# Cross-attention and MoE feed-forward: the q and k parts go into the score stacks straight from SBUF instead of through DRAM

## The chip, the cores and the metric

One core of a Trainium2 chip runs the whole kernel. The metric is device time in microseconds (us) for one execution, as the median of several runs. Engines are called TensorE (PE in the profile, with PEld for its weight loads), VectorE (DVE), ScalarE (ACT), GpSimd (POOL) and SyncE (SP). SyncE does no arithmetic: it issues the DMA transfers, one after the other, and a wait in its stream holds everything behind it.

## The reference

x and ctx have 16 batches of 128 rows of 256. The first layer is attention with 16 query heads of 16 and one shared key/value head:

```
x  = layernorm(x)
qh = (x @ w_q)  -> 16 heads of 16;   k, v = ctx @ w_kv   (16 each)
x  = x + concat_heads(softmax(qh k^T / 4) v) @ w_concat
```

The second is a top-1 mixture of 8 experts (256 -> 1024 -> 256, gelu, 256 rows of capacity each) beside a residual MLP of the same shape. The two outputs are mixed by a softmax of two learned coefficients and added to the residual. Everything is in f32, and the score product must keep nearly f32 accuracy.

## The kernel before

**Tiles.** The 16 batches make U = 8 tiles ("u") of T = 2 batches ("t"), 256 rows. A tile passes through layer norm, transposes, the k/v and q products, the scores, the softmax, PV, the projection, the gate, a scatter of its rows to the experts' slots in DRAM, and the residual MLP. After the last tile the 8 experts run.

**Stacks.** q and k are each split into three bf16 parts (high, middle, low), made in SBUF as `qpart` (128 partitions: 16 dimensions d times 8 head pairs h) and `kpart` (16 partitions). The six products of parts that matter are put side by side along the contraction: `qstack` and `kstack` have 96 = 6 x 16 rows of parts, row 16a + d holding dimension d of copy a, plus two rows for the running maximum. The high q part fills copies 0 to 2, the middle 3 and 4, the low 5; the k copies are 0, 1, 2, then 0, 1, then 0. One matmul over 96 rows then gives a score. The fold of 128 partitions (d, h) into 16 rows of 8 heads needs DMA.

**How the stacks are filled before.** `k_spill(u)` (L434) writes kpart to DRAM in three transfers. `q_spill(u, i)` (L445) waits for part i (q_hi, q_mid, q_parts) and writes it to DRAM, three, two and one times over, by one transfer each. `gather(u, i)` (L455) waits until those have landed (and, from tile 2 on, until the second scores of tile u - 2 no longer need the buffer), and reads all 96 rows of kstack by one transfer and of qstack by one for each of the two batches. All stacks and parts are double-buffered by u % 2.

**Who uses them.** `score_max` on TensorE (step "A", L696) multiplies groups g = 0 to 7 (four heads each, the first four groups for batch 0) and VectorE takes the maxima of each (L1064). The maxima are transposed (step "M", L708), negated and split in two, and `maxima` on SyncE (L467) puts them into the last two rows of qstack. Then `scores_T` (step "B", L718) computes the transposed scores, 98 rows deep, and ScalarE takes the exponential (L904). Tile 0 does its maxima in two halves, the others in one. `k_parts` on GpSimd (L548) and `q_first` on ScalarE (L882) overwrite kpart and qpart of the tile before last.

**Order.** There is no scheduler at run time. Every engine runs one fixed stream. The order of each stream is worked out when the kernel is built: each step has a planned time (tables AT0, AT1, AT for tiles 0, 1 and the rest, relative to the tile's own time OWN[u]) and each engine adds a lag per kind (LAG_SP for SyncE and so on); sorting gives the stream. On SyncE the resulting order around the first tiles is: loads, q_spill 0 of tile 0, k_spill of tile 0, q_spill 1 and 2, load of tile 3, gather 0 of tile 0, q_spill 0 and k_spill and q_spill 1 and 2 of tile 1, gather 1 of tile 0, gather 0 of tile 1, maxima of tile 0 (first half), gather 1 of tile 1, maxima of tile 0 (second half), load of tile 4, the zeroing of the experts' slots. From tile 4 on it is: maxima of tile u - 1, q_spills 0 to 2 of tile u, k_spill, the two gathers, then output rows, weights and a load.

On TensorE the order of tile 1's first scores is: second half of tile 0's A, M of tile 0, A 0 and 1 of tile 1, context transposes of tile 2, A 2 of tile 1, B 0 of tile 0, k/v product of tile 2, and on in this manner.

Of the kernel before, what the change touches and what calls it, by code (L numbers as in the profile page):

```python
# [5 lines left out]
def xattn_moe_ffn_kernel(nc, x, ctx, w_q, w_kv, w_c, nw, nb, wg, inter_w, inter_b, output_w, output_b,  # L6
# [4 lines left out]
    bf16 = mybir.dt.bfloat16  # L11
# [14 lines left out]
    T = 2  # L26
# [23 lines left out]
    out_v = out.rearrange("(b p) d -> b p d", p=P)  # L50


    dram_q = nc.dram_tensor("dram_q", [2, REP, P, KC * UT], bf16).ap()
    dram_k = nc.dram_tensor("dram_k", [2, REP, DH, UT], bf16).ap()
    disp = nc.dram_tensor("dispatched", [E * CAP + S, ROW], f32).ap()


# [3 lines left out]
    while len(OWN) < U + 3:  # L61
# [9 lines left out]
        "down": [0.08, 0.92, 1.12, 2.02, 7.51, 10.4, 27.63, 33.31], "kspill": [-40.85],  # L71
        "qspill": [-47.2, -43.78, -37.85], "gather": [-34.62, -27.72],
    }
    AT1 = {
        "load": [-99.9], "ln1": [-77.08], "xn": [-50.43], "ctxT": [-48.78], "xT": [-41.65], "kv": [-46.17],
# [5 lines left out]
        "down": [-2.72, -1.63, 2.04, 2.67, 8.58, 11.01, 13.67, 16.13], "kspill": [-26.77],  # L81
        "qspill": [-33.14, -29.81, -29.17], "gather": [-40.06, -39.06],
    }
    AT = {
        "load": [-98.82], "ln1": [-69.02], "xn": [-48.54], "ctxT": [-48.69], "xT": [-41.01], "kv": [-46.16],
# [5 lines left out]
        "down": [-3.91, -1.52, 1.85, 2.78, 6.17, 12.14, 13.12, 15.62], "kspill": [-25.95],  # L91
        "qspill": [-34.54, -33.37, -31.71], "gather": [-39.81, -38.61],
    }
    EARLY = 0.01
    LAG_PE = {
# [16 lines left out]
        "bias": [-5.5], "down": [0.38], "qlast": [-0.2], "end": [-0.84], "small": [-0.06], "ws1": [1.57],  # L112
    }
    LAG_SP = {
        "load": [-4.81], "kspill": [-5.64], "qspill": [-0.35], "gather": [13.54], "M": [3.71], "wload": [0.2],
        "ein": [1.22], "down": [7.99], "zero": [3.09], "late": [0.29], "w1load": [-0.02], "end": [-0.43],
        "small": [0.55], "w2load": [0.66],
    }
# [19 lines left out]
    for u in range(U):  # L138
        at = (AT0, AT1, AT)[min(u, 2)]
        for kind in ("load", "ln1", "xn", "ctxT", "xT", "kv", "q", "qrest", "qmid", "qlast", "vt", "oT", "proj", "ln2",  # L140
                     "core", "gate", "loc"):
            if kind != "load" or u >= 2:
                add(OWN[u] + at[kind][0], kind, u)
        free = OWN[u - 2] + 14.6 if u >= 2 else -100
        add(max(OWN[u] + at["kspill"][0], free), "kspill", u)
        for i, phase in enumerate(at["qspill"]):
            add(max(OWN[u] + phase, free + 0.1 * (i + 1)), "qspill", u, i)
        for i in range(T):
            add(max(OWN[u] + at["gather"][i], free + 0.5 + 0.1 * i), "gather", u, i)
        for i in range(T - HALVES[u], T):  # L150
            add(OWN[u] + at["M"][i], "M", u, i + HALVES[u] - T)
        for kind in ("A", "B", "PV", "part", "o"):
            for i, phase in enumerate(at[kind]):
                add(OWN[u] + phase, kind, u, i)
        weighed = max(OWN[u + 1] + at["gw"][0] if u + 1 < U else 0, OWN[u] + at["loc"][0] + 0.1)
        add(weighed, "gw", u)
        add(max(OWN[u + 1] + at["bias"][0], weighed + 0.1), "bias", u)
        for c, phase in enumerate(at["up"]):
            add(OWN[u + 1] + phase, "up", u, c)
        for i, phase in enumerate(at["down"]):  # L160
            t, q = divmod(i, 4)
            add(OWN[u + 1] + PERIOD + (phase if u >= 2 else at["down"][4 * t] + EARLY * q), "down", u, t, q)
# [23 lines left out]
    with ExitStack() as ex:  # L186
# [187 lines left out]
        def _(sp):  # L374
# [56 lines left out]
                w1load(e)  # L431
                w2load(e)

            def k_spill(u):  # L434
                r = u % 2
                sp.wait_ge(sem("k_parts"), u + 1)
                if u >= 2:
                    sp.wait_ge(sem(f"stack_in{r}"), 16 * (u // 2))
                row = 0
                for parts in (3, 2, 1):  # L440
                    sp.dma_start(dram_k[r, row:row + parts].rearrange("a d t -> d a t"), kpart[:, r, 0:parts, :])\
                      .then_inc(sem(f"k_spill{r}"), 16)
                    row += parts

            def q_spill(u, i):  # L445
                r, (name, row, times) = u % 2, (("q_hi", 0, 3), ("q_mid", 3, 2), ("q_parts", 5, 1))[i]
                sp.wait_ge(sem(name), u + 1)
                if u >= 2:
                    for t in range(T):
                        sp.wait_ge(sem(f"q_in{r}{t}"), 16 * (u // 2))  # L450
                sp.dma_start(dram_q[r, row:row + times].rearrange("a p c -> p a c"),
                             qpart[:, r, i, :, :, :].rearrange("p t m x -> p (t m x)").unsqueeze(1)
                             .broadcast_to([P, times, T * KC * P])).then_inc(sem(f"q_spill{r}"), 16)

            def gather(u, i):  # L455
                r = u % 2
                if i == 0:
                    if u >= 2:
                        sp.wait_ge(sem("b_done"), G * (u - 1))
                    sp.wait_ge(sem(f"k_spill{r}"), 3 * 16 * (u // 2 + 1))  # L460
                    sp.dma_start(kstack[0:KS, r, :], dram_k[r].rearrange("a d t -> (a d) t")).then_inc(sem(f"stack_in{r}"), 16)
                    sp.wait_ge(sem(f"q_spill{r}"), 3 * 16 * (u // 2 + 1))
                sp.dma_start(qstack[0:KS, r, i, :, :].rearrange("r (h m) x -> r h (m x)", m=KC),
                             dram_q[r].rearrange("a (d h) (t c) -> t (a d) h c", d=DH, t=T)[i])\
                  .then_inc(sem(f"q_in{r}{i}"), 16)

            def maxima(u, i):  # L467
                sp.wait_ge(sem("m_split"), max_steps(u, i) + 1)
# [24 lines left out]
            def end():  # L493
                sp.wait_ge(sem("acc_out"), 16 * (NBATCH + 1))

            calls = {"small": small, "late": late, "zero": zero, "load": load, "wload": wload, "w1load": w1load, "w2load": w2load, "kspill": k_spill, "qspill": q_spill, "gather": gather, "M": maxima, "ein": expert_in,
                     "down": down, "end": end}
            for step in order(LAG_SP):
                if step[0] in calls:
# [3 lines left out]
        def _(pool):  # L503
# [44 lines left out]
            def k_parts(u):  # L548
                pool.wait_ge(sem("kv_copied"), u + 1)
                if u >= 2:  # L550
                    pool.wait_ge(sem(f"k_spill{u % 2}"), 3 * 16 * (u // 2))
                k = kpart[:, u % 2, :, :]
                own(pool.tensor_copy(k[:, 0, :], kv32[0:DH, :]))
                own(pool.tensor_tensor(kres[:, :], kv32[0:DH, :], k[:, 0, :], ALU.subtract))
                own(pool.tensor_copy(k[:, 1, :], kres[:, :]))
                pool.tensor_tensor(k[:, 2, :], kres[:, :], k[:, 1, :], ALU.subtract).then_inc(sem("k_parts"), 1)
# [77 lines left out]
        def _(pe):  # L634
# [61 lines left out]
            def score_max(u, g):  # L696
                r, t, bs = u % 2, g // HG, slice((g // HG) * P, (g // HG + 1) * P)
                if g == 0:
                    pe.wait_ge(sem(f"stack_in{r}"), 16 * (u // 2 + 1))
                if g % HG == 0:  # L700
                    pe.wait_ge(sem(f"q_in{r}{t}"), 16 * (u // 2 + 1))
                b = claim("A", u, g)
                for i in range(4):
                    last = nc.tensor.matmul(b[:, i * P:(i + 1) * P], qstack[0:KS, r, t, 4 * (g % HG) + i, :],  # L704
# [147 lines left out]
        def _(act):  # L852
# [29 lines left out]
            def q_first(u):  # L882
                act.wait_ge(sem("q_done"), u + 1)
                if u >= 2:
                    act.wait_ge(sem(f"q_spill{u % 2}"), 3 * 16 * (u // 2))
                copy(qpart[:, u % 2, 0, :, :, :], by_batch(place["q", u])).then_inc(sem("q_hi"), 1)

            def q_second(u):
# [359 lines left out]
```

## Time and profile before

| | |
|---|---|
| median of 3 runs | 373.2 us (372.02 to 373.33) |
| the profiled execution | 374.39 us, span of the core 372.7 us |
| TensorE busy | 340.6 us, 91% of the span |
| VectorE / ScalarE / GpSimd busy | 56% / 58% / 43% |
| DMA: moved, mean rate | 49.83 MB, 134 GB/s |
| SyncE transfers for the stacks, per tile | 3 k spills, 3 q spills, 1 k gather, 2 q gathers |

The span is the time from the first to the last instruction of the core in the profile; the time of the execution also holds what lies around it. A row of a timeline has a start (us), a duration (us), the engine, the line of the kernel, the operation, the tile written and the tiles read, a count where several are merged, and in brackets how long the engine stood idle before and what ended that. For SyncE (SPq) the duration is that of the issue alone; the data lands later.

### The profile page before, as it was taken

The numbers are of one execution on the slowest core, as the hardware profiler recorded it, in microseconds if no ns is written. First come the engines' busy times: TensorE is split into PE (matmuls) and PEld (weight loads), VectorE is DVE, ScalarE is ACT, GpSimd is POOL, SyncE is SP. The second block draws the span as 40 slices with busy tenths as digits, with TensorE's granted clock in tenths as the row PEclk, the third lists the DMA queues.
The fourth block names the chain that finished last, engine by engine and source line by source line (L and its number), as shares of the span: only waits on it lengthen the run. The fifth ranks groups of instructions, "written<-read, shape, count | busy, mean of one in ns | idle before, by whom it ended". The sixth has DMA issues, their size and how long they took to land.

```text
span 372.7 us, 6349 instructions
## 1 busy us (share of the span) xinstructions
PE 340.6 (91%) x2234; PEld 277.6 (74%) x2234; DVE 207.8 (56%) x533; ACT 217.9 (58%) x397; POOL 160.5 (43%) x219
## 2 busy tenths in 40 slices
PE   3748889999999999999999989989999999999990
PEld 2425545875885885886786776778899999999990
DVE  4255528843762673574475462422668977878550
ACT  3311376484474465456447346363799999999730
POOL 4430233369657446636735542446002443334232
PEclk9965599999999999999999999999999999999996
DMA  6665539381224306706804400102936987875122
GB/s 183 197 202 144 166 106 315 117 230 60 79 82 116 99 28 179 261 2 176 288 2 133 107 2 15 44 1 66 295 84 182 279 272 189 233 199 140 17 30 28
DMA packets 51336, 49.83 MB, mean 134 GB/s; under 512 B 4765, under 2 KB 48489, under 8 KB 51305
## 3 DMA queue, kind: packets, MB, share of 16 engines
q1 hardware_dynamic: 48232, 45.21, 40.4%
q0 software_dynamic: 3072, 4.21, 6.1%
q8 instruction: 18, 0.29, 0.3%
q14 instruction: 14, 0.11, 0.1%
HBM read 33.65 MB, written 15.63 MB: 132 GB/s over the span
## 4 chain that ended last, share of the span: by engine, by line
PE 83%; DVE 5%; ACT 4%; issue 2%; DMA 2%; SPq 1%; POOL 1%; POOLq 0%; DVEq 0%
PE ubank L651 25%; PE mbank L833 16%; PE mbank L651 12%; PE mbank L646 4%; PE mbank L839 4%; PE mbank L840 4%; PE mbank L838 4%; PE pbank L736 4%; PE sbank L704 4%; PE sbank L726 4%; DVE smax L1069 2%; PE pbank L745 2%; DMA qstack<-dram_q 1%; DMA wq_raw<-in_L_xattn_w_q 1%; ACT h L976 1%
## 5 line engine op out<-in xcount | busy, mean ns | idle before, releaser
L976 ACT ACTIVATE h<-ubank,vecT 128x256 f32<-128x256 f32 x128 | 53.1, 467 | 29.8 <-PE ubank L651 29.7
L619 POOL DMA_INDIRECT out_rows<-yrow,rowid x16 | 32.3, 2017 | 74.0 <-DVE yrow L1213 74.0
L833 PE MATMUL mbank<-w2r,h 128*128 128x256 f32 x256 | 61.6, 383 | 1.5 <-ACT h L976 0.7
L651 PE MATMUL ubank<-ao,w1r 128*128 128x256 f32 x256 | 60.4, 382 | 0.0
L1069 DVE TENSOR_REDUCE smax<-sbank 128x4 f32<-128x512 f32 x64 | 42.5, 686 | 21.1 <-PE sbank L704 20.7
L833 PEld LDWEIGHTS mbank<-w2r,h 128*128 128x128 f32 x256 | 47.1, 190 | 9.3 <-issue 1.6
L651 PEld LDWEIGHTS ubank<-ao,w1r 128*128 128x128 f32 x256 | 46.8, 190 | 5.8
L910 ACT ACTIVATE p<-sbank 128x512 f32<-128x512 f32 x64 | 35.7, 596 | 15.7 <-PE sbank L726 15.5
L838 PE MATMUL mbank<-w2h,hh 128*128 128x256 f32 x128 | 36.4, 285 | 0.0
L840 PE MATMUL mbank<-w2h,hl 128*128 128x256 f32 x128 | 36.0, 281 | 0.0
L839 PE MATMUL mbank<-w2l,hh 128*128 128x256 f32 x128 | 36.0, 281 | 0.0
L704 PE MATMUL sbank<-kstack,qstack 96*128 96x128 bf16 x256 | 26.1, 236 | 5.9 <-DVE smax L1069 2.8
L704 PEld LDWEIGHTS sbank<-kstack,qstack 96*128 96x128 bf16 x256 | 19.3, 105 | 16.2 <-issue 6.5
L651 PE MATMUL ubank<-aoh,w1h 128*128 128x256 f32 x128 | 26.3, 286 | 0.0
L651 PE MATMUL ubank<-aol,w1h 128*128 128x256 f32 x128 | 25.6, 281 | 0.0
L651 PE MATMUL ubank<-aoh,w1l 128*128 128x256 f32 x128 | 25.6, 281 | 0.0
L568 POOL TENSOR_TENSOR yy<-va,mhalf 128x4 f32<-128x4 f32 x8 | 8.3, 1043 | 38.5 <-DVE va L1106 38.5
L839 PEld LDWEIGHTS mbank<-w2l,hh 128*128 128x128 f32 x128 | 24.2, 189 | 0.0
L838 PEld LDWEIGHTS mbank<-w2h,hh 128*128 128x128 f32 x128 | 24.2, 189 | 0.0
L840 PEld LDWEIGHTS mbank<-w2h,hl 128*128 128x128 f32 x128 | 24.2, 189 | 0.0
L726 PE MATMUL sbank<-qstack,kstack 98*128 98x512 bf16 x64 | 22.5, 396 | 1.6 <-ACT p L910 1.4
L1191 DVE TENSOR_TENSOR hl<-h,hh 128x512 fp32r<-128x512 f32 x32 | 21.9, 687 | 1.8 <-ACT hh L854 1.8
(139 smaller groups left out, 668.4 us busy)
## 6 DMA issues: line engine op xcount, KB each, us to landing
w1e<-in_L_ffn_inter_w SPq DMA_DIRECT2D x8, 1024.0 KB, 6.6
w2e<-in_L_ffn_output_w SPq DMA_DIRECT2D x8, 1024.0 KB, 7.9
qstack<-dram_q SPq DMA_DIRECT2D x16, 384.0 KB, 4.7
dram_q<-qpart SPq DMA_DIRECT2D x8, 384.0 KB, 2.6
dispatched<-zrow SPq DMA_DIRECT2D x4, 516.0 KB, 6.1
drow<-dispatched SPq DMA_DIRECT2D x8, 258.0 KB, 7.6
xs<-in_x SPq DMA_DIRECT2D x8, 256.0 KB, 3.2
ctxs<-in_ctx SPq DMA_DIRECT2D x8, 256.0 KB, 3.4
```

The lines of the kernel that those rows point to most:

```text
L619: pool.indirect_dma_start(out=out[:, :], in_=yrow[:, e % 2, t, :], in_offset=None, compute_op=ALU.add, out_offset=bass.IndirectOffsetOnAxi ...
L651: last = nc.tensor.matmul(dst, w[kc], v[kc], start=(kc == 0), stop=(kc == len(w) - 1))
L704: last = nc.tensor.matmul(b[:, i * P:(i + 1) * P], qstack[0:KS, r, t, 4 * (g % HG) + i, :], kstack[0:KS, r, bs], start=True, stop=True)
L726: nc.tensor.matmul(b[:, :], kstack[:, r, bs], qstack[:, r, t, hs:hs + 4, :], start=True, stop=True)\
L833: last = nc.tensor.matmul(b[:, 0:D], h[:, n % 2, f, t * P:(t + 1) * P], w2[:, f, :], start=(f == 0), stop=(f == FC - 1))
L838: nc.tensor.matmul(b[:, 0:D], hi, wh, start=(f == 0), stop=False)
L839: nc.tensor.matmul(b[:, 0:D], hi, wl, start=False, stop=False)
L840: last = nc.tensor.matmul(b[:, 0:D], lo, wh, start=False, stop=(f == FC - 1))
L910: nc.scalar.activation(p32[:, (k // HB) % 2, g % HB, :, :], scores, ACT.Exp, scale=SCALE)\
L976: nc.scalar.activation(h[:, n % 2, f, :], place["up", n, c][:, j, :], ACT.Gelu_apprx_tanh, bias=vecT[:, col:col + 1]).then_inc(sem("gelu_d ...
L1069: V.reduce_max(smax[:, g // HG, hs:hs + 4], place["A", u, g][:, :].rearrange("p (h t) -> p h t", h=4), AX)\
L1191: V.tensor_tensor(hl[:, n % 2, 2 * c:2 * c + 2, :], a, hh[:, n % 2, 2 * c:2 * c + 2, :].bitcast(f32), ALU.subtract)\
```

## The change

The two DRAM tensors go, and so does the step "gather". In the places of k_spill and q_spill in every order stand `k_stack` and `q_stack`, which write the stacks directly: 6 transfers of 8 KB for k and 6 + 4 + 2 transfers of 64 KB for q in each tile. The wait for the second scores of tile u - 2, which stood ahead of the gather, now stands ahead of these. The semaphores that TensorE waits for count six transfers, and k_parts and q_first wait for the stack transfers of tile u - 2 in place of the spills.

```diff
-    dram_q = nc.dram_tensor("dram_q", [2, REP, P, KC * UT], bf16).ap()
-    dram_k = nc.dram_tensor("dram_k", [2, REP, DH, UT], bf16).ap()
...
-        for i in range(T):
-            add(max(OWN[u] + at["gather"][i], free + 0.5 + 0.1 * i), "gather", u, i)
...
-            def k_spill(u):
-                r = u % 2
+            def k_stack(u):
+                r, row = u % 2, 0
                 sp.wait_ge(sem("k_parts"), u + 1)
                 if u >= 2:
-                    sp.wait_ge(sem(f"stack_in{r}"), 16 * (u // 2))
-                row = 0
+                    sp.wait_ge(sem("b_done"), G * (u - 1))
                 for parts in (3, 2, 1):
-                    sp.dma_start(dram_k[r, row:row + parts].rearrange("a d t -> d a t"), kpart[:, r, 0:parts, :])\
-                      .then_inc(sem(f"k_spill{r}"), 16)
-                    row += parts
-
-            def q_spill(u, i):
+                    for i in range(parts):
+                        sp.dma_start(kstack[row:row + DH, r, :], kpart[:, r, i, :]).then_inc(sem(f"stack_in{r}"), 16)
+                        row += DH
+
+            def q_stack(u, i):
                 r, (name, row, times) = u % 2, (("q_hi", 0, 3), ("q_mid", 3, 2), ("q_parts", 5, 1))[i]
                 sp.wait_ge(sem(name), u + 1)
                 if u >= 2:
+                    sp.wait_ge(sem("b_done"), G * (u - 1))
+                for a in range(row, row + times):
                     for t in range(T):
-                        sp.wait_ge(sem(f"q_in{r}{t}"), 16 * (u // 2))
...
+                        sp.dma_start(qstack[a * DH:(a + 1) * DH, r, t, :, :].rearrange("d (h m) x -> d h (m x)", m=KC),
+                                     qpart[:, r, i, t, :, :].rearrange("p m x -> p (m x)"))\
+                          .then_inc(sem(f"q_in{r}{t}"), 16)
...
-                    pool.wait_ge(sem(f"k_spill{u % 2}"), 3 * 16 * (u // 2))
+                    pool.wait_ge(sem(f"stack_in{u % 2}"), REP * 16 * (u // 2))
...
-                    pe.wait_ge(sem(f"stack_in{r}"), 16 * (u // 2 + 1))
+                    pe.wait_ge(sem(f"stack_in{r}"), REP * 16 * (u // 2 + 1))
                 if g % HG == 0:
-                    pe.wait_ge(sem(f"q_in{r}{t}"), 16 * (u // 2 + 1))
+                    pe.wait_ge(sem(f"q_in{r}{t}"), REP * 16 * (u // 2 + 1))
...
-                    act.wait_ge(sem(f"q_spill{u % 2}"), 3 * 16 * (u // 2))
+                    for t in range(T):
+                        act.wait_ge(sem(f"q_in{u % 2}{t}"), REP * 16 * (u // 2))
```

## Rows read from the trace of the kernel before

**Rows 1.** Page, 40 slices of the span: TensorE busy in tenths, and its granted clock.
```profile
PE   3748889999999999999999989989999999999990
PEclk9965599999999999999999999999999999999996
```

**Rows 2.** Chain that ended last, 0 to 70 us: start us, length us, what.
```profile
20.75 0.61 ACT qpart L854
...
24.37 3.99 DMA qstack<-dram_q
...
29.05 0.70 DVE smax L1069
```

**Rows 3.** Timeline of SyncE, tile 0: start us, issue us, line, operation.
```profile
13.03 0.37 SPq L451 DMA_DIRECT2D dram_q<-qpart  x1
...
14.57 0.42 SPq L441 DMA_DIRECT2D dram_k<-kpart  x1
...
16.02 0.45 SPq L410 DMA_DIRECT2D xs<-in_x  x1
...
17.66 0.66 SPq L463 DMA_DIRECT2D qstack<-dram_q  x1
```

**Rows 4.** By source line: issue ns min/median/max, and for two lines issue to landing.
```profile
L463 SPq DMA_DIRECT2D qstack<-dram_q x16: 547/616/1192, 17.7 to 202.9; - x16
...
DMA to landing us min/median/max: 4.0/4.7/6.3
...
L472 SPq DMA_DIRECT2D qstack<-nmax x14: 514/562/894, 47.3 to 221.6; - x14
...
DMA to landing us min/median/max: 1.8/1.9/2.2
...
L441 SPq DMA_DIRECT2D dram_k<-kpart x24: 312/420/1425, 13.4 to 200.4; - x24
```

**Rows 5.** Timeline of TensorE, tiles 0 and 1.
```profile
17.42 3.29 PE L651 MATMUL mbank<-xT,wq 128*128 128x256 f32 x8 [0.78 <-ACT xT L854]
22.03 0.61 PE L704 MATMUL sbank<-kstack,qstack 96*128 96x128 bf16 x8 [1.32 <-DMA qstack<-dram_q]
...
28.41 1.03 PE L704 MATMUL sbank<-kstack,qstack 96*128 96x128 bf16 x8 [1.50 <-DMA qstack<-dram_q]
...
32.05 1.06 PE L704 MATMUL sbank<-kstack,qstack 96*128 96x128 bf16 x8
...
34.23 0.59 PE L726 MATMUL sbank<-qstack,kstack 98*128 98x512 bf16 x1
```

**Rows 6.** Timeline: a q product at each clock; one window (clock, DMA share, GB/s last).
```profile
41.61 3.73 PE L651 MATMUL mbank<-xT,wq 128*128 128x256 f32 x8
...
64.84 1.95 PE L651 MATMUL mbank<-xT,wq 128*128 128x256 f32 x8
...
45.00:46.00 1.00, 0.78 (x6) 0.31 (x4) 0.41 (x1) 0.63 (x2) 0.00 (x0) 0.90 0.00 0
```

**Rows 7.** Timelines around tile 2's stack: second scores of tile 0, SyncE, first scores.
```profile
47.61 0.39 PE L726 MATMUL sbank<-qstack,kstack 98*128 98x512 bf16 x1 [0.47 <-ACT p L910]
...
48.61 1.44 SPq L441 DMA_DIRECT2D dram_k<-kpart  x3
...
59.77 0.40 PE L704 MATMUL sbank<-kstack,qstack 96*128 96x128 bf16 x4
```

**Rows 8.** Timelines of tiles 5 and 6: first q transfer on SyncE, first scores on TensorE.
```profile
138.01 0.52 SPq L451 DMA_DIRECT2D dram_q<-qpart  x1
...
150.92 0.39 PE L704 MATMUL sbank<-kstack,qstack 96*128 96x128 bf16 x4
...
166.65 2.79 SPq L451 DMA_DIRECT2D dram_q<-qpart  x3
...
179.85 0.39 PE L704 MATMUL sbank<-kstack,qstack 96*128 96x128 bf16 x4
```

More of the change, by code:

```diff
@@ L71, in xattn_moe_ffn_kernel @@
         "down": [0.08, 0.92, 1.12, 2.02, 7.51, 10.4, 27.63, 33.31], "kspill": [-40.85],
-        "qspill": [-47.2, -43.78, -37.85], "gather": [-34.62, -27.72],
+        "qspill": [-47.2, -43.78, -37.85],
     }
@@ L81, in xattn_moe_ffn_kernel @@
         "down": [-2.72, -1.63, 2.04, 2.67, 8.58, 11.01, 13.67, 16.13], "kspill": [-26.77],
-        "qspill": [-33.14, -29.81, -29.17], "gather": [-40.06, -39.06],
+        "qspill": [-33.14, -29.81, -29.17],
     }
@@ L91, in xattn_moe_ffn_kernel @@
         "down": [-3.91, -1.52, 1.85, 2.78, 6.17, 12.14, 13.12, 15.62], "kspill": [-25.95],
-        "qspill": [-34.54, -33.37, -31.71], "gather": [-39.81, -38.61],
+        "qspill": [-34.54, -33.37, -31.71],
     }
@@ L114, in xattn_moe_ffn_kernel @@
     LAG_SP = {
-        "load": [-4.81], "kspill": [-5.64], "qspill": [-0.35], "gather": [13.54], "M": [3.71], "wload": [0.2],
+        "load": [-4.81], "kspill": [-5.64], "qspill": [-0.35],  "M": [3.71], "wload": [0.2],
         "ein": [1.22], "down": [7.99], "zero": [3.09], "late": [0.29], "w1load": [-0.02], "end": [-0.43],
@@ L448, in q_spill @@
                 if u >= 2:
+                    sp.wait_ge(sem("b_done"), G * (u - 1))
+                for a in range(row, row + times):
                     for t in range(T):
-                        sp.wait_ge(sem(f"q_in{r}{t}"), 16 * (u // 2))
[L451 to L465, printed above, removed]
+                        sp.dma_start(qstack[a * DH:(a + 1) * DH, r, t, :, :].rearrange("d (h m) x -> d h (m x)", m=KC),
+                                     qpart[:, r, i, t, :, :].rearrange("p m x -> p (m x)"))\
+                          .then_inc(sem(f"q_in{r}{t}"), 16)
             def maxima(u, i):
@@ L494, in end @@
                 sp.wait_ge(sem("acc_out"), 16 * (NBATCH + 1))
-            calls = {"small": small, "late": late, "zero": zero, "load": load, "wload": wload, "w1load": w1load, "w2load": w2load, "kspill": k_spill, "qspill": q_spill, "gather": gather, "M": maxima, "ein": expert_in,
+            calls = {"small": small, "late": late, "zero": zero, "load": load, "wload": wload, "w1load": w1load, "w2load": w2load, "kspill": k_stack, "qspill": q_stack, "M": maxima, "ein": expert_in,
                      "down": down, "end": end}
```

## The prediction, made before the changed kernel was run

> **What bounds the kernel now.** I read the page first: TensorE is busy 91% of 372.7 us, and the slices show where it is not: the first four or five (9.3 us each), which also hold the stretch at half the granted clock, and the very end [rows 1]. From about 60 us on the chain that ended last is almost all TensorE work. So this change can only matter in two ways: through the first 35 us, where TensorE still waits for data, or by making a later tile's stack come too late. The chain of waits for the first 70 us names the place: the q copy of tile 1 on ScalarE, then SyncE issues, then a q gather, then the first score matmuls of tile 0's second half at 28.41, and from there TensorE, VectorE and ScalarE hand work to each other without another transfer for q or k on the path [rows 2, 5]. The gather at 24.37 belongs to tile 0: SyncE's order puts it behind a wait for tile 1's q, and it only lands at 28.4.
>
> Then I read SyncE's own timeline. A transfer costs the queue 0.37 to 0.66 us of issue and a gap of about 0.04 to the next, whatever its size: 8 KB at 14.57 takes 0.42, 256 KB of x 0.45 [rows 3]. This is the price to which the change adds: nine issues a tile before (three k spills, three q spills, three gathers by my count in the code), eighteen after, in one stream on one queue.
>
> **Price of one new transfer.** No row has exactly the new q form (128 source partitions of 512 bytes into 16 partitions of 8 rows). Two rows bound it: the maxima, which also go SBUF to SBUF and fold source partitions into a row of the destination (median 0.562 us of issue, 1.9 us from issue to landing, 8 KB), and the q gather (median 0.616, 4.7 to landing, 384 KB) [rows 4]. 64 KB and folding put it next to the maxima: I take 0.57 + 0.04 = 0.61 us of queue and 2.1 us to landing, with 0.46 (the 0.42 of the k spill at 14.57, plus gap) and 0.70 (the 0.66 at 17.66) as ends [rows 3]. The new k form is plain, 16 partitions to 16: 0.43 + 0.04 = 0.47, by the k spills' median of 0.420 [rows 4], and 2.0 to landing, next to the maxima's 1.9; the ends are 0.46 and, if it costs what the maxima cost, 0.60. A tile then needs S = 12 x 0.61 + 6 x 0.47 = 10.1 us of SyncE, with ends 8.3 and 12.0.
>
> **Tile 0.** SyncE is free at 13.03, as before. q_hi takes 3.66 us (to 16.69), k 2.82 (to 19.51), q_mid 2.44 (to 21.95); the first transfer of q_parts, which completes the first half, starts there and lands at 24.05. The first score matmul moves from 22.03 [rows 5] to 24.05, 2.0 later. The second half lands 0.6 later, though, and not at 28.4. After four matmul groups, which VectorE reads at 0.70 us each [rows 2], it can start near 28.0 against 28.41. So tile 0 as such gives back its delay and gains 0.4; its last maxima transpose stands near 31.5 instead of 31.89.
>
> **Tile 1, the term that decides.** Its stack starts when SyncE has issued tile 0's eighteen (13.03 + 10.14 = 23.17) and the two loads of tile 3 (1.0 us: the 0.45 at 16.02 twice, with gaps [rows 3]): 24.17. Its q_hi has been ready since 21.4 [rows 2], so nothing is waited for. Then 3.66 + 2.82 + 2.44 = 8.92 us: at 33.09 the first q_parts transfer goes out, and it lands at 35.2. TensorE took tile 1's first scores at 32.05, without a wait for data [rows 5]. That is 35.2 - 32.05 = +3.1 us. In general the start is 14.03 + 2S - 2q + 2.1 with q the price of one q transfer: each 0.1 us more a transfer costs 3.4 us here. What follows in TensorE's fixed order (context transposes, kv, q of tile 2, the second scores) moves with it.
>
> **The maxima of tile 0** stand behind all of this on SyncE. Their first pair comes at 34.35 (24.17 + 10.14 and the gap); the second of the pair starts 0.6 later and lands near 37.0. The second scores of tile 0 want it: they ran at 34.23, 2.2 after tile 1's first scores [rows 5], so now at 37.4. It is covered by 0.4, and costs nothing more. The maxima of the second half follow within 2 us and are wanted only after tile 2's q product, which ends at 45.3 [rows 6].
>
> **Does it last?** From 32 us on the chain has no event at a fixed time: every step waits for a TensorE, VectorE or ScalarE step ahead of it [rows 2]. So I let the 3.1 us run through to the end. The granted clock is half, 1.2 GHz, in the slices between 25 and 45 us [rows 1] and rises early in the microsecond from 45 to 46, as the uninterrupted q product of tile 2 ends [rows 6]. That product keeps its place in the order and so moves with the rest; I put the clock at zero, with 1 us to either side (the same eight matmuls take 3.73 us at the lower level and 1.95 at the higher, [rows 6], so half a product at the other level).
>
> **Tiles 2 to 7.** The k and q steps now wait for the second scores of two tiles before, where only the gather did. For tile 2 those end at 48.0 and SyncE comes at 48.61 [rows 7]; for later tiles they are a whole tile in the past. So the wait costs nothing while SyncE stays behind it; behind it would stand only the stack itself. Tile 2: 48.61 + 2.82 + 6.10 = 57.53, landing 59.6, wanted at 59.77 [rows 7]: covered by 0.2. Tiles 3 and 4 have several microseconds more cover than those behind them. In tiles 5 to 7 the stack starts right behind the maxima: 138.01 + 10.14 - 0.47 = 147.7 for the last k issue, landing 149.7, wanted at 150.92 [rows 8], 1.2 us of cover; tile 6 runs from 166.65 to 179.85 in the same way, 1.5 us of cover [rows 8], and tile 7 as tile 6. What is queued behind (expert weights, output rows, the next x) goes out 3 to 4 us later. The expert weights are taken up only after the last tile's projection (the waits for x1_ready in split and split2), the output rows by nobody, the next x more than half a period later: nothing there is on the path. One more pair of waits on ScalarE's q_first and the later release of the k buffer on GpSimd look at transfers landed a tile earlier: nothing.
>
> **What is removed.** The DRAM round trip (the spill's landing and the gather's 4.7 us [rows 4]) goes, and with it what it wrote to HBM and read back in each tile. In tiles 2 to 7 that stood off the path; in tile 0 it is in the sum above.
>
> **Sum.** +3.1 us on the span: 375.8. The profiled execution took 374.39 for a span of 372.7, 1.2 above the median of 373.2; with the same 1.7 around the span the changed one would be 377.5 by its own profile, and 373.2 + 3.1 = 376.3 as a median.
>
> The Trainium skill (SBUF, State Buffer, section on the DMA port swizzle) says that partitions 0 to 15 reach only four of sixteen ports and gives 104 GB/s for them; a new q transfer writes 16 partitions. As an estimate from that page, 64 KB would take 0.63 us to write; landing would be some 0.5 us later and the sum 3.6. No row of the kernel before shows so narrow a write of this size.
>
> **Rivals.**
> *Cheap issues.* If the new transfers issue like the cheapest k spills (0.46 a piece), S = 8.3 and tile 1's first scores could start at 14.03 + 16.6 - 0.9 + 2.1 = 31.8: not later than now. Time 373.2, and within 0.5% (about what a measurement of this kernel can tell from no change, 1.9 us) up to S = 9.5. For: plain forms cost that in [rows 3]. Against: both forms of [rows 4] that go into the q stack have a minimum above 0.51. Chance 0.23.
> *The stack becomes the period.* SyncE's round is maxima, stack, landing, first scores, maxima. From S = 11.4 on it no longer fits: 138.01 + 11.4 - 0.5 + 2.0 = 150.9. At S = 12.0 tile 1 is 14.03 + 24.0 - 1.4 + 2.1 = 38.7 (+6.7), tile 2 61.3 (+1.5), tiles 5, 6 and 7 +0.5, +0.2 and +0.2: +9.1 us, 382.3. For: single issues of 0.66 us and, in a k spill, up to 1.43 are there [rows 3, 4], and a narrow write may hold the queue back. Against: the medians. Chance 0.15.
> *Faster.* If issuing cost next to nothing and only landings counted, tile 0's stack (all its parts are out on SyncE before the load at 16.02 [rows 3]) would be there at 16.0 + 2.1 = 18.1, before TensorE ends tile 1's q product at 20.7 [rows 5]. Then the first scores start 1.3 earlier and the wait of 1.5 before 28.41 [rows 5] goes too: -2.8 us, 370.4. For: the chain did hold that gather. Against: SyncE's own rows, where issues stand end to end at half a microsecond each. Chance 0.07. The Trainium skill (DMA: Bandwidth & Descriptors, section "Issuing engines are not separate DMA queues") calls issue time usually small relative to the DMA itself; by that rule this rival would be the forecast. The same page's rules for kernel authors advise coalescing small transfers, which speaks for the forecast.
>
> **How the numbers follow.** The forecast (375.1 to 378.9, S from about 9.5 to 11.4) has 0.55, the rivals 0.23, 0.15 and 0.07. Slower by over 0.5%: 0.55 + 0.15 minus the forecast's lower edge, where the clock could take one back: 0.68. Within: 0.25. Faster: 0.07. The range of 372.6 to 382.0 leaves out the faster rival and half of the period rival, 0.15.
>
> **What would show it.** Right: in SyncE's timeline after 13.03 eighteen issues in 10 us, the second tile's from about 24 to 34; first scores at about 24.0 (tile 0) and 35.2 (tile 1), with the wait before the latter ended by a stack transfer; cover left in tiles 5 to 7 and a period of 28.9 us between their first scores, as now. Wrong: issues under 0.5 us (then the first rival), waits for stack transfers in tiles 5 to 7 (the second), first scores of tile 1 before 32 us (the third), or a stretch of the lower clock longer or shorter by several microseconds, on which the sum has nothing.

## The result, and the profile after

The changed kernel takes 390.2 us (median of four runs, 389.5 to 390.5) against 373.3 before: ratio 1.043, 95% interval 1.035 to 1.051. It is 16.9 us slower where 3.1 were forecast, outside the range.

The page of the changed kernel: its span, TensorE's busy slices and clock, and the shares of the chain that ended last.

```profile
span 388.7 us, 6415 instructions
...
PE   4733877996999999999999998989999999999991
...
PEclk9955799899699999999999999999999999999997
...
PE 69%; SPq 10%; DMA 5%; issue 5%; DVE 4%; ACT 2%; POOL 2%; POOLq 0%; DVEq 0%
```

Against [rows 1] there is a third thin place: a low clock in the eleventh slice, around 100 us, long after the start. And SyncE's queue (SPq) holds 10% of the chain; before it held 1%.

SyncE's timeline, tiles 0 and 1 (start, duration, count of merged issues); it answers to [rows 3].

```profile
13.63 3.88 SPq L447 DMA_DIRECT2D qstack<-qpart  x6
17.55 3.75 SPq L437 DMA_DIRECT2D kstack<-kpart  x6
21.35 3.80 SPq L447 DMA_DIRECT2D qstack<-qpart  x6
25.19 0.59 SPq L406 DMA_DIRECT2D xs<-in_x  x1
...
26.34 3.76 SPq L447 DMA_DIRECT2D qstack<-qpart  x6
30.14 3.75 SPq L437 DMA_DIRECT2D kstack<-kpart  x6
33.94 3.80 SPq L447 DMA_DIRECT2D qstack<-qpart  x6
37.78 2.49 SPq L459 DMA_DIRECT2D qstack<-nmax  x4
```

Eighteen issues stand end to end from 13.63 to 25.15, 11.5 us, and again from 26.34 to 37.74. By source line (issue in ns, min/median/max), with the landing of the q transfers:

```profile
L437 SPq DMA_DIRECT2D kstack<-kpart x48: 528/589/599, 17.6 to 222.7; - x48
...
L447 SPq DMA_DIRECT2D qstack<-qpart x96: 546/598/1831, 13.6 to 218.8; - x96
...
DMA to landing us min/median/max: 2.4/2.6/3.0
```

An 8 KB k transfer holds the queue as long as a 64 KB q transfer, 0.59 and 0.60 us. TensorE's timeline shows the places where time is lost; these answer to [rows 5], [rows 7] and [rows 8]. (The wait before 26.75 is tile 0's; its delay disappears in the longer wait before 39.30. A last one, 0.61 us, stands before tile 7's first scores at 224.93.)

```profile
26.75 1.01 PE L688 MATMUL sbank<-kstack,qstack 96*128 96x128 bf16 x8 [5.87 <-DMA qstack<-qpart]
...
39.30 1.01 PE L688 MATMUL sbank<-kstack,qstack 96*128 96x128 bf16 x8 [5.00 <-DMA qstack<-qpart]
...
47.23 1.95 PE L635 MATMUL mbank<-xT,wq 128*128 128x256 f32 x8
...
65.86 0.38 PE L688 MATMUL sbank<-kstack,qstack 96*128 96x128 bf16 x4 [2.17 <-issue]
...
72.12 1.95 PE L635 MATMUL mbank<-xT,wq 128*128 128x256 f32 x8
...
98.06 6.77 PE L817 MATMUL mbank<-w2r,h 128*128 128x256 f32 x16 [3.66 <-DVE xs L1188]
104.76 1.06 PE L720 MATMUL pbank<-p,vone 128*32 128x512 f32 x8
...
166.27 0.40 PE L688 MATMUL sbank<-kstack,qstack 96*128 96x128 bf16 x4 [0.93 <-DMA kstack<-kpart]
```

The account of the span, read as the distance between the same instruction in the traces. The second column is the trace of before_zero_early (see the experiments), a kernel whose instructions are those of the kernel before, with one step of SyncE moved that nothing waited for:

| where | before | before_zero_early | after | behind before | behind before_zero_early |
|---|---|---|---|---|---|
| first scores of tile 1 | 32.05 | 33.04 | 39.30 | 7.25 | 6.3 |
| q product of tile 2 (and its duration) | 41.61 (3.73) | 41.28 (1.95) | 47.23 (1.95) | 5.6 | 5.95 |
| first maxima transfer of tile 1 | 47.34 | 45.24 | 51.19 | 3.85 | 5.95 |
| first scores of tile 2 | 59.77 | 57.67 | 65.86 | 6.1 | 8.2 |
| q product of tile 3 | 64.84 | 62.74 | 72.12 | 7.3 | 9.4 |
| PV behind the second down product of tile 0 | 90.52 | 88.41 | 104.76 | 14.2 | 16.35 |
| first scores of tile 5 | 150.92 | 148.82 | 166.27 | 15.35 | 17.45 |
| span | 372.7 | 370.7 | 388.7 | 16.0 | 18.0 |

Two things in these columns are not the change's doing. SyncE's first stack transfer starts anywhere from 12.6 to 15.0 us in the traces of this case (13.03 before, 14.41 in before_zero_early, 13.63 after). And the execution profiled before, at 374.4 us a slower one than its median of 373.2, had the low clock until 45 us: 1.0 us ahead of before_zero_early at tile 1's first scores, it was 2.1 behind by tile 1's first maxima transfer.

The row at 98.06 is the largest single loss: TensorE stands 3.66 us for VectorE's xs, and the 16 matmuls then take 6.77 us. Before, the same 16 took 3.62 without a wait. Who is late shows on GpSimd's timeline, first of the kernel before (with TensorE's down product from its own timeline below it), then of the changed one (the number in brackets is the idle time and what ended it):

```profile
81.32 1.25 POOL L596 DMA_INDIRECT dispatched<-core,slot  x1 [0.65 <-POOL core L590]
84.90 0.73 POOL L606 TENSOR_TENSOR xs<-xs,rbias 128x256 f32<-128x256 f32 x1
...
86.97 3.62 PE L833 MATMUL mbank<-w2r,h 128*128 128x256 f32 x16
```

```profile
93.08 1.25 POOL L580 DMA_INDIRECT dispatched<-core,slot  x1 [5.13 <-DMA dispatched<-zrow]
...
96.66 0.72 POOL L590 TENSOR_TENSOR xs<-xs,rbias 128x256 f32<-128x256 f32 x1
```

GpSimd's scatter of tile 0's rows waits for the fourth zeroing of the experts' slots. That transfer stands on SyncE behind tile 3's stack: issued at 76.0 before, at 87.5 now, 11.5 us later, while TensorE was 7.3 behind. Behind the scatter, on GpSimd's own stream, stands the bias that VectorE needs before it can empty the bank that TensorE wants. The scatter's idle time grew from 0.65 to 5.13 us, by 4.5, of which TensorE felt 3.66: 0.8 us was covered. I had called everything behind the stack free.

### The profile page after: what moved, and what is told of

Its sections match the earlier page's. It is cut to its first block, busy times and chain, and to the rows that moved or that the text cites. A ratio compares the mean times of both kernels' runs of the same rounds, so it can differ in the third digit from the quotient of the medians.

```text
span 388.7 us, 6415 instructions
## 1 busy us (share of the span) xinstructions
PE 342.4 (88%) x2234; PEld 278.8 (72%) x2234; DVE 207.8 (53%) x533; ACT 217.8 (56%) x397; POOL 160.4 (41%) x219
## 4 chain that ended last, share of the span: by engine, by line
PE 69%; SPq 10%; DMA 5%; issue 5%; DVE 4%; ACT 2%; POOL 2%; POOLq 0%; DVEq 0%
PE ubank L635 21%; PE mbank L817 12%; PE mbank L635 10%; SPq L447 6%; PE mbank L630 4%; PE mbank L823 4%; PE mbank L824 4%; PE mbank L822 4%; PE sbank L688 4%; SPq L437 3%; PE pbank L720 3%; PE sbank L710 2%; PE pbank L729 2%; DVE smax L1054 2%; DMA dispatched<-zrow 1%
## 5 line engine op out<-in xcount | busy, mean ns | idle before, releaser
L817 PE MATMUL mbank<-w2r,h 128*128 128x256 f32 x256 | 64.8, 398 | 5.1 <-DVE xs L1188 3.7
L817 PEld LDWEIGHTS mbank<-w2r,h 128*128 128x128 f32 x256 | 49.1, 198 | 14.1 <-DVE xs L1188 4.2
L1188 DVE SCALAR_TENSOR_TENSOR xs<-mbank,coef,xs 128x256 f32<-128x256 f32 x16 | 7.7, 484 | 29.7 <-PE mbank L817 20.1
```

What stands on the lines that cost most here:

```text
L817: last = nc.tensor.matmul(b[:, 0:D], h[:, n % 2, f, t * P:(t + 1) * P], w2[:, f, :], start=(f == 0), stop=(f == FC - 1))
```

## The experiments

Each is compared with runs of the kernel before on the same chip; its median was 372.2 to 372.5 us there.

### The zeroing alone

```diff
-        "late": [-158.95], "vec": [21.72], "zero": [-0.17, 2.25, 6.33, 40.44],
+        "late": [-158.95], "vec": [21.72], "zero": [-0.17, 2.25, 6.33, 32.6],
```

On the changed kernel:

> The changed kernel with one step of SyncE moved: the fourth zeroing of the experts' slots (planned time 40.44 made 32.6) is issued ahead of tile 3's stack instead of behind its eighteen transfers. Theory (a step behind the stack that I had costed at nothing): TensorE's stall of 3.66 us at 94.4 to 98.06, ended by VectorE's xs, which waits for GpSimd, which waits 5.13 us for the zeroing, goes, and so does the half clock of the 16 down matmuls behind it (6.77 us instead of 3.62): 6.8 us less, about 383.4. Rival (the scatter of tile 0 is late for another reason, or the next wait is just behind): under 2 us less, above 388.

Measured: 383.98 us, ratio 1.033 (1.028 to 1.038), 6.2 us less than the changed kernel's 390.2. The two were not measured side by side; each against its own kernel before, they are 16.9 and 11.8 us slower, which makes it 5.1. The theory holds: the wait for xs is gone from TensorE's list.

The same line on the kernel before:

> The kernel before with the same step moved in the same way. Theory: there the zeroing is issued at 76.0 and GpSimd waits 0.65 us for it with TensorE not waiting at all, so nothing changes: 373.2, within 0.5 us. Rival (the place of the zeroing is a loss in itself): 1 us or more less.

Measured: 372.82 against 372.17, ratio 1.004 (1.000 to 1.008): nothing gained. GpSimd still stands 0.65 us idle before the scatter, as it does in zero_early, so that idle time was never a wait for the zeroing, as my expectation had it. The place of the zeroing costs only once something long stands ahead of it.

### The price of an issue by itself

```diff
+                group("pr_narrow", [(d, src) for d in narrow])
+                group("pr_wide", [(d, src) for d in wide])
+                group("pr_store", [(scr[i], src) for i in range(12)])
+                group("pr_load", [(d, scr[i]) for i, d in enumerate(wide)])
+                group("pr_loadn", [(d, scr[i]) for i, d in enumerate(narrow)])
+                group("pr_small", [(d, xs[0:DH, 0, 0:P]) for d in small])
+                group("pr_smalls", [(scr[i, 0:DH], xs[0:DH, 0, 0:P]) for i in range(REP)])
+                group("pr_smalll", [(d, scr[i, 0:DH]) for i, d in enumerate(small)])
```

> The kernel before, with groups of transfers added at the end of SyncE's stream, each group back to back and waited for: twelve of 64 KB SBUF to SBUF into 16 partitions of 8 rows, twelve into 128 partitions, twelve to DRAM, twelve back into 128 partitions, twelve back into 16; six of 8 KB SBUF to SBUF, to DRAM, and back. They measure the disputed price alone. Theory (an issue with both sides in SBUF costs 0.59, one with a side in DRAM about 0.45, whatever the size or the number of partitions): first, second and sixth group 0.59, the others 0.42 to 0.47. Rival (the 16-partition destination is what costs): first, fifth, sixth and eighth group at 0.59, the others lower. A second question: if a write into 16 partitions runs at a quarter of the rate, the first and fifth group land later after the last issue than the second and fourth, by 0.5 us or more; else they land alike.

The program as a whole took 390.7 us, which says nothing, as the groups were put at its end. One line issues them all; the view by source line (issue in ns, min/median/max) parts them by what they move between, and the timeline gives the two groups of 64 KB and the small ones.

```profile
L500 SPq DMA_DIRECT2D xs<-xs x30: 520/601/1806, 330.8 to 379.3; - x30
L500 SPq DMA_DIRECT2D xs<-scr x30: 303/422/468, 360.7 to 386.9; - x30
L500 SPq DMA_DIRECT2D scr<-xs x18: 308/432/491, 353.8 to 383.2; - x18
...
342.74 7.64 SPq L500 DMA_DIRECT2D xs<-xs  x12
...
353.79 5.66 SPq L500 DMA_DIRECT2D scr<-xs  x12
...
376.12 3.73 SPq L500 DMA_DIRECT2D xs<-xs  x6
381.04 2.62 SPq L500 DMA_DIRECT2D scr<-xs  x6
384.71 2.62 SPq L500 DMA_DIRECT2D xs<-scr  x6
```

Twelve transfers of 64 KB between 128 partitions, both sides in SBUF, take 7.64 us, 0.64 each; twelve to DRAM 5.66, 0.47 each. Six of 8 KB: 3.73 and 2.62, so 0.62 and 0.44. The group that has the changed kernel's form, twelve into 16 partitions, took 9.43 us, with the same median issue of 0.602 but one of 1.81. Between 8 and 64 KB and between 16 and 128 partitions the median does not move; both sides in SBUF raise it. The theory holds for these forms and the rival falls. It is no general rule that a side in DRAM makes an issue cheap: the q gathers of the kernel before, 384 KB from DRAM, have a median of 0.616 [rows 4]. Why it is so, no run shows.

The second question, landing. DMA issues in two windows: the twelve loads into 128 partitions (with one of the next group), then the twelve into 16 (KB each, median us from issue to landing).

```profile
xs<-scr SPq DMA_DIRECT2D x13, 64.0 KB, 2.3
...
xs<-scr SPq DMA_DIRECT2D x12, 64.0 KB, 3.0
```

The narrow write lands 0.7 us later. The Trainium skill (SBUF, State Buffer, section on the DMA port swizzle) has four of sixteen ports for 16 partitions, from which the prediction worked out 0.5 us as an estimate; the measured 0.7 is of that size. For the two groups with both sides in SBUF the profile gives no landing.

### One part at a time

k straight, q by DRAM as before:

```diff
-                    sp.dma_start(dram_k[r, row:row + parts].rearrange("a d t -> d a t"), kpart[:, r, 0:parts, :])\
-                      .then_inc(sem(f"k_spill{r}"), 16)
-                    row += parts
+                    for i in range(parts):
+                        sp.dma_start(kstack[row:row + DH, r, :], kpart[:, r, i, :]).then_inc(sem(f"stack_in{r}"), 16)
+                        row += DH
```

> Only the k parts go straight (six transfers), q stays by DRAM (three spills, two gathers). Theory (time of SyncE's queue, 0.59 us plus 0.04 for every SBUF to SBUF transfer into 16 partitions, whatever its size): k takes 3.8 us of queue instead of 2.0, tile 0's and tile 1's data come about 2.2 us later, the zeroing about 2 us later, of which 0.8 is covered: +2 to +4, 375 to 377. Rival (the q writes of 64 KB into 16 partitions are what is slow, the k part is free): 373 to 374.

Measured: 378.78 us, ratio 1.018 (1.013 to 1.024), 6.6 us more than before and 2 us above the expectation. Its trace says which term: tile 1's first scores are at 35.19 (its stream started 0.5 us later, so 2.6 behind, near the 2.2 expected), but the second down product of tile 0 loses more than a stall:

```profile
90.13 5.35 PE L829 MATMUL mbank<-w2r,h 128*128 128x256 f32 x16 [1.99 <-DVE xs L1199]
```

2.0 us of stall and 1.7 us of a longer product: the granted clock was 1.2 GHz from 90.1 to 93.5. Moving 48 KB a tile in a shorter way cost 1.8%.

q straight, k by DRAM:

```diff
-                sp.dma_start(dram_q[r, row:row + times].rearrange("a p c -> p a c"),
-                             qpart[:, r, i, :, :, :].rearrange("p t m x -> p (t m x)").unsqueeze(1)
-                             .broadcast_to([P, times, T * KC * P])).then_inc(sem(f"q_spill{r}"), 16)
+                for a in range(row, row + times):
+                    for t in range(T):
+                        sp.dma_start(qstack[a * DH:(a + 1) * DH, r, t, :, :].rearrange("d (h m) x -> d h (m x)", m=KC),
+                                     qpart[:, r, i, t, :, :].rearrange("p m x -> p (m x)"))\
+                          .then_inc(sem(f"q_in{r}{t}"), 16)
```

> Only the q parts go straight (twelve transfers), k stays by DRAM (three spills, one gather). Theory (queue time): 12 x 0.63 + 3 x 0.47 + 0.4 = 9.4 us a tile instead of 11.4; tile 1's first scores at about 34.7 (+2.6 on the kernel before), the zeroing about 2 us later than before with 0.8 covered: +3 to +5, 376 to 378. Rival (the q writes are slow in the DMA engines, so that taking k away helps little): above 384.

Measured: 378.60 us, ratio 1.020 (1.014 to 1.027), 0.6 above the theory's upper end. Tile 1's first scores are at 37.21, not at 34.7; 1.95 us of that is a stream that started later (14.98). What they wait for is not q but the k gather, which stands behind all the q transfers on the queue. The wait for xs is 1.0 us, and the product behind it takes 3.72 us, at the full clock. Both halves of the change lose by themselves, and by about the same, though q moves sixteen times the bytes of k.

### Queue time without the change's data

Nine transfers of 1 KB that nobody reads were added to the kernel before; here for tile 3 (the other kernel has (0, 1) in its place):

```diff
                     row += parts
+                if u in (3,):
+                    sp.wait_ge(sem("route_const"), 5)
+                    for j in range(9):
+                        sp.dma_start(dum[:, (3,).index(u), j, :], tri[0:DH, 0:32]).then_inc(sem("dum"), 16)
```

> The kernel before with nine extra transfers of 1 KB (16 partitions, 64 bytes each, SBUF to SBUF, to a spare tile that nobody reads) on SyncE behind tile 3's k spills, ahead of the fourth zeroing; nothing else. Theory (queue time alone, and a step that stands behind it): the zeroing goes out 9 x 0.63 = 5.7 us later, GpSimd's scatter waits for it, VectorE's xs waits for GpSimd, TensorE stalls about 4.9 us at the down product of tile 0 (5.7 less 0.8 of cover), and if it then runs 3 us at half clock the loss is 8: 378 to 381. Rival (the zeroing was late in the changed kernel because of the DMA engines' load, not of the queue): under 2 us.

Measured: 380.21 us, ratio 1.020 (1.016 to 1.025). SyncE's timeline and TensorE's, of this kernel:

```profile
74.12 6.01 SPq L448 DMA_DIRECT2D dum<-tri  x9
80.18 0.58 SPq L403 DMA_DIRECT2D dispatched<-zrow  x1
...
89.98 6.48 PE L838 MATMUL mbank<-w2r,h 128*128 128x256 f32 x16 [4.73 <-DVE xs L1208]
```

Nine kilobytes cost 7.8 us: 4.7 of stall (4.9 expected) and a down product of 6.48 us in place of 3.62. This is the loss of the changed kernel at 98 us, made with nothing of the change in it. In all four kernels in which the scatter waits for the zeroing, its idle time beyond 0.65 us is 0.8 more than TensorE's stall: 4.5 and 3.7 in the changed kernel, 5.6 and 4.7 here, 2.8 and 2.0 in k_direct_only, 1.8 and 1.0 in q_direct_only.

> The kernel before with the same nine extra transfers, this time behind the k spills of tile 0 and of tile 1, so that SyncE has as many issues there as in the changed kernel (eighteen a tile) while the data goes its old way. Theory (queue time): tile 0's first scores at about 27.7 as in the changed kernel, tile 1's at about 38, 5 to 6 us later than before; part of it is given back because the clock rises earlier: 375 to 379. Rival (it is the form or the data of the new transfers): under 1.5 us.

Measured: 382.35 us, ratio 1.025 (1.021 to 1.029): 9.9 us, more than the theory's 3 to 7. TensorE's timeline:

```profile
30.45 1.01 PE L709 MATMUL sbank<-kstack,qstack 96*128 96x128 bf16 x8 [9.47 <-DMA qstack<-dram_q]
...
39.89 1.03 PE L709 MATMUL sbank<-kstack,qstack 96*128 96x128 bf16 x8 [5.61 <-DMA qstack<-dram_q]
...
43.53 1.06 PE L709 MATMUL sbank<-kstack,qstack 96*128 96x128 bf16 x8
```

The mechanism is the expected one and its size was not: here the gather of tile 0's second half still waits behind tile 1's queue, so tile 0 loses time that the changed kernel does not, and tile 1's first scores start at 43.53. That is 10.5 us behind before_zero_early, and 9.9 is what the run costs: hardly any of it was given back, where my expectation had the clock return a part. Queue time alone is enough for the loss at the start, and more.

### Fewer and larger transfers

With the stack laid out so that the two batches of a head pair are neighbours, one q transfer carries both (the zeroing is early as in zero_early; in this layout each half of tile 0's maxima takes four transfers instead of two):

```diff
-    qstack = sb("qstack", [KS + 2, 2, T, NH, P], bf16, att)
+    qstack = sb("qstack", [KS + 2, 2, NH // KC, T, KC, P], bf16, att)
...
-                    for t in range(T):
-                        sp.dma_start(qstack[a * DH:(a + 1) * DH, r, t, :, :].rearrange("d (h m) x -> d h (m x)", m=KC),
-                                     qpart[:, r, i, t, :, :].rearrange("p m x -> p (m x)"))\
-                          .then_inc(sem(f"q_in{r}{t}"), 16)
+                    sp.dma_start(qstack[a * DH:(a + 1) * DH, r].rearrange("d h t m x -> d h (t m x)"),
+                                 qpart[:, r, i].rearrange("p t m x -> p (t m x)"))\
+                      .then_inc(sem(f"q_in{r}"), 16)
```

> The changed kernel with the stack laid out so that one q transfer carries both batches (128 KB in rows of 1 KB; six q and six k transfers a tile instead of twelve and six), four instead of two transfers for each half of tile 0's maxima, and the fourth zeroing early as in zero_early. Theory (queue time by the number of transfers): 12 x 0.63 = 7.6 us a tile instead of 11.4; tile 1's first scores near 32 to 33; 373 to 375. Rival (data into 16 partitions, not issues, is the limit; bytes are the same): tile 1's first scores still after 36 and the time near zero_early's, above 380.

Measured: 376.32 us, ratio 1.011 (1.003 to 1.018), 7.7 us less than zero_early with the same bytes over the same path. Tile 1's first scores are at 33.87 (in zero_early 40.29). The rival falls. The time is 1.3 us above the theory's upper end. A 128 KB transfer lands after a median of 4.0 us, where the 64 KB one took 2.6, and the maxima of tile 0 hold the queue for 5.55 us instead of 2.49; which of them costs the 1.3 is not shown.

The same with k back in DRAM, where four cheap issues replace six dear ones:

> q straight from SBUF by six transfers of 128 KB a tile (the layout of merged_zero), k through DRAM as before (three spills, one gather), zeroing early. Queue time of a tile by the measured prices: 6 x 0.64 + 3 x 0.47 + 0.43 = 5.7 us (before 4.3, merged_zero 7.6). Theory: tile 1's first scores near 31 to 32, no wait for the stack in later tiles: 371 to 373, equal to the kernel before or just faster. Rival (a straight q transfer is worse than the DRAM way for another reason too, such as its landing of 3.9 us): 375 or more.

Measured: 371.89 us against 372.46, ratio 0.998 (0.995 to 1.001): no difference that can be told. It is the best version that sends q straight, and its queue time of a tile, 5.7 us, is near that of the kernel before (4.8 for tile 0 by its issues from 13.03 on, gaps included; the expectation had 4.3).

### The gather that was on the chain

```diff
-        "qspill": [-47.2, -43.78, -37.85], "gather": [-34.62, -27.72],
+        "qspill": [-47.2, -43.78, -37.85], "gather": [-34.62, -34.5],
```

> The kernel before with one step moved: the gather of tile 0's second half is issued right behind that of the first half instead of behind the wait for tile 1's q. Theory: the wait of 1.5 us ahead of 28.41 goes, the rest of tile 0's first scores is bound by VectorE, and 1 to 1.5 us come off: 371 to 372 where the kernel before has 372.2 to 373.3. Rival (tile 1's spills and gathers, which come behind it, are then as late as before, and bind): no change.

Measured: 373.16 us, ratio 1.001 (0.998 to 1.005). The wait ahead of tile 0's second half is gone from its trace, and nothing is gained that can be told. This is the kernel before with the one wait removed that the prediction had put at 1.5 us in its faster rival. It is not removed for free: with two gathers of 384 KB out together, tile 0's first scores start 10.2 us after the stream's first transfer, against 9.0 to 9.4 in the traces that keep the old order.

## Why the prediction was wrong, point by point

**What bounds: right.** TensorE is late for stacks in tiles 0 and 1, and later tiles are a matter of cover. SyncE's queue, not the data, sets both.

**The price of a transfer: q right, k mis-sized.** q was put at 0.57 + 0.04, measured 0.598 + 0.04. k was put at 0.47 because the k spills cost that; measured 0.589 + 0.04. The spills have one side in DRAM, and the new transfer has none: the row to read was the maxima's, also for k. I had it as an upper end (0.60) and dismissed it because the form "is plain". This is 6 x 0.16 = 1.0 us of S. Together with 12 x 0.03 for q, S was 11.5 instead of 10.1, above the point of 11.4 that the period rival names.

**Tile 0: right in form.** Its first scores moved to 26.75, not 24.05, and its second half followed without a wait for data, as predicted.

**Tile 1: the formula right, its input not.** With S = 11.5, q = 0.64, a landing of 2.6 and a stream that begins 0.6 us later (13.63 for 13.03), 14.63 + 23.0 - 1.3 + 2.6 = 38.9; measured 39.30. The term was +7.25 where I had +3.1, or 6.65 when each trace is counted from its own first stack transfer. The landing was 0.5 short (median 2.6 for 2.1), as the sentence on the narrow write had it.

**Does it last: right. The clock: no part of the change at the start, a missing term later.** Against the profile before, half of the 7.25 seems to be given back at once, since tile 2's q product took 1.95 us instead of 3.73. That is an accident of the execution that was profiled. The windows (clock third from the right) of the changed kernel, of before_zero_early and of zero_early:

```profile
42.00:43.00 1.00, 1.00 (x4) 0.60 (x4) 0.32 (x1) 0.60 (x1) 0.00 (x0) 0.59 1.03 290
43.00:44.00 1.00, 0.99 (x8) 0.28 (x5) 0.19 (x1) 0.38 (x1) 0.08 (x1) 1.00 0.87 302
```

```profile
37.00:38.00 1.00, 1.00 (x7) 0.28 (x5) 0.15 (x1) 0.38 (x1) 0.03 (x1) 0.94 1.04 351
...
41.28 1.95 PE L651 MATMUL mbank<-xT,wq 128*128 128x256 f32 x8
...
45.24 1.14 SPq L472 DMA_DIRECT2D qstack<-nmax  x2
```

```profile
44.00:45.00 1.00, 1.00 (x5) 0.24 (x4) 0.00 (x0) 0.06 (x1) 0.00 (x0) 0.51 1.01 333
```

Up to here before_zero_early runs the same instructions in the same order as the kernel before, and still its clock rose at 37.1 and not at 45.1; zero_early runs those of the changed kernel, and its clock rose at 45.0 and not at 42.8. Against before_zero_early the loss runs on undiminished, 6.3 us at tile 1's first scores and 5.95 behind them, so letting it run through was right. What TensorE did just before does not settle the moment either: it was busy without a gap from 39.3 in the changed kernel and rose within 4 us, and from 31.9 to 37.7 in the profile before without rising.

Later stalls cost more than their length. Around the waits of 2.17 us before 65.86 and of 3.66 before 98.06 the level was 1.2 GHz for 3.4 us (from 66.7) and for 6.8 us (from 97.4). The second stall cost 3.66 + 3.15 us, nearly twice its length; the one of 1.0 us in q_direct_only cost hardly more than its length.

**Tiles 2 to 7: the covers were gone.** Tile 2 had 0.2 us of cover by my sum and was 2.2 us late; S = 11.5 and the longer landing give 1.6 of it. Tile 5 had 1.2 and was 0.93 late, tile 7 was 0.61 late, and tile 6 was not late. S = 11.5 uses up the cover, no more: it is in tiles 5 and 7 that the twelve q issues took 8.90 and 8.52 us instead of 7.67, with single issues of up to 1.83.

**The steps that failed.** Two. The first is the sentence "nothing there is on the path", on what is queued behind the stack. I went through weights, output rows and x loads, and left out the fourth zeroing, which stands in SyncE's order behind tile 3's stack. (My description of the order names the zeroing only behind the load of tile 4, where the first three stand.) It has a reader, GpSimd's scatter, with bias and so VectorE and TensorE behind it. The cover was there to be read: VectorE's xs ends at 86.26 (start 85.78, 0.48 long), TensorE's product starts at 86.97, 0.7 us later, near the 0.8 that the four kernels show. The missing step is 5 to 6 us by zero_early, about a third of the loss, and nine kilobytes of other traffic reproduce it. The second is the price of a transfer, of k's above all, a mis-sized term: without the zeroing the kernel still takes 384.0 us, 11.8 more than before and outside the range. Those 11.8 are S = 11.5 where I had 10.1, the landing, and what follows from them in tiles 1, 2, 5 and 7, with the lower clock behind tile 2's stall.

**The rivals.** "The stack becomes the period" was nearest, at 382.3 with a chance of 0.15; it is about what zero_early shows (384.0), that is, the change without the step that I had missed. "Cheap issues" and "faster" fall with the probe. The rule of the Trainium skill that issue time is usually small relative to the DMA (DMA: Bandwidth & Descriptors, "Issuing engines are not separate DMA queues") misleads for this stream: one issue of 0.60 us is still less than the 2.6 us to landing, but landings overlap and issues do not, and eighteen of them set the pace. The advice of the same page of the Trainium skill (Rules for kernel authors) to coalesce small transfers agrees with merged_zero, 7.7 us.

**Open.** No run held the clock fixed, and what moves its rise by 8 us between executions of the same instructions is not shown. Nor is what made single issues take up to 1.83 us. Why a transfer between two SBUF sides holds the queue longer is not shown either.

## What to carry to other kernels

Count a transfer by its issue first: on one queue, eighteen small direct transfers are slower than nine that go through DRAM, and the price is to be taken from a row with the same ends and form, not from one that merely looks as plain. When a step in a queue grows, list every step behind it with its reader and that reader's slack, the dull ones too; the one left out cost 5 to 6 us. Stalls of 2.0 to 4.7 us in an otherwise dense stretch of TensorE cost up to twice their length here, by the half-clock time around them. And before a gain or loss of a microsecond or two is read from two traces, a second trace of the same kernel is worth having.

## What the runs showed of the hardware that I had not expected

An issue on SyncE's queue took a median of 0.60 us with both sides in SBUF and 0.42 to 0.43 with one in DRAM, for 8 KB as for 64 KB, for 16 partitions as for 128 (probe). Writing 64 KB from DRAM into 16 partitions lands 0.7 us later than into 128. And the same instructions in the same order met the rise of the clock at 45.1 us in one execution and at 37.1 in another, with spans of 372.7 and 370.7 us. Near the start, the clock is not the same from one execution to the next.
